# Layer one's passage between turns: a projection added sooner, key values ahead of query columns, the shift and more maxima ahead of the scores

## The chip, the cores and the metric

The kernel runs on one core of one Trainium2 chip. A core has five engines that run their own instruction streams: TensorE (PE, matmuls and transposes), VectorE (DVE), ScalarE (ACT), GpSimd (POOL) and SyncE (SP, which issues DMAs here). They meet at semaphores. The metric is the device time of one execution in microseconds (us). TensorE, VectorE and ScalarE share PSUM, eight banks of 128 x 512 f32 elements: TensorE writes a bank, another engine reads it and so makes it free.

## What is computed

Four layers, each a cross attention and a feed-forward part, act on `x` of 4 batches x 256 tokens x 256. Only layer one's attention is touched by the change. Cut to that:

```python
def _L1_xattn_ref(q, latent_kv, Wq, Wkv_expand, Wout):
    B, S, H, NH, L = (2, 256, 256, 16, 64)
    HD = H // NH
    qp = q @ Wq.T
    kv = latent_kv @ Wkv_expand.T
    k, v = jnp.split(kv, 2, axis=-1)
    # heads: (b, 16, 256, 16)
    scores = jnp.einsum('bhqd,bhkd->bhqk', qh, kh) * inv_sqrt_d
    scores = jnp.where(causal, scores, jnp.finfo(scores.dtype).min)
    attn = jax.nn.softmax(scores, axis=-1)
    out = jnp.einsum('bhqk,bhkd->bhqd', attn, vh)
    return out @ Wout.T

x = x + jnp.tanh(g_xattn[1]) * _L1_xattn_ref(_layernorm(x, axis=-1), ctx_512, ...)
```

## The kernel before

The stage of layer one's attention (its names end in `1`, its bank plan is `l1x`) takes the four batches in two turns, `i` = 0 and 1, of two batches, `s` = 0 and 1. In a turn:

- Queries (L1473) and key values (L1481) are made on TensorE. ScalarE, VectorE and GpSimd split them into bf16 parts: `query_parts1`, `key_parts1` on ScalarE (L2160) and VectorE (L2821 to L2873), the second batch's on GpSimd (L968, L970).
- TensorE turns the parts into columns (L1188): `qsT` and `ksT` for the first batch, four fills of eight transposes each, `cols` for the second, four fills of sixteen. ScalarE moves turned queries (L2040), VectorE turned keys of the first batch (L2835).
- 12 fills with scores for each batch, `max1(i, s, k)` (L1408 and the mask L1410), are reduced to maxima by VectorE (`maximum1`, L2882). Fills with k under 4 hold four heads (8 matmuls), the others two heads (4 matmuls).
- The shift made from the maxima (L2888, L2890) is turned by TensorE (`shift1`, L1188 with 32 rows), copied (L2896) and put by a DMA of SyncE (L812) into two more rows of the operands.
- `exp1(i, s, m)`, 8 fills for each batch (L1421, L1423), makes the scores once more, now less the shift; ScalarE takes the exponential (L2206); `values1` (L1439) multiplies it by the values. Then come tokens, turned heads (`turn_heads`) and the projection (`project`, L1464), which VectorE adds to x (`add_projected`, L2914). The projection of batch (0,1) is made in the second turn, after its first shift; that of (0,0) at the end of the first turn.

The order of the engines' work is written out by hand. `max_order1(i)` gives the order of maxima ahead of the scores, `AHEAD1` how many of the second batch's maxima are among them, and `rest_at1` after which scores the others go. `plan` assigns the fills of a group to banks in rotation: group M takes banks 6, 7, 4, 5; group A banks 4 and 5; B the pairs 0-1 and 2-3; V the pair 6-7. A fill waits until the one before it in its bank has been read. TensorE works in order, so what stands behind a waiting fill waits with it. VectorE fills spare time with pieces of another layer's work, `advance(largest, n)` (L2709, L2714, L2721).

Of the kernel before, what the change touches and what calls it, by code (L numbers as in the profile page):

```python
# [171 lines left out]
def flamingo_gated(nc, x, ctx_512, g_xattn, g_ffn, W_k0, b_k0, ln_gamma, ln_beta, gate_w, gate_b, expert_w, expert_b,  # L172
                   Wq1, Wkv1, Wout1, w_gate, w_up, w_down, Wq2, Wk2, gamma_raw, w12, w3, router_w, expert_bias,
                   sw1, sw2, sw3, W_router, W_sgate, Ws_gate_up, Ws_down, We_gate_up, We_down, consts, out):
    with ExitStack() as ctx:
# [350 lines left out]

        AHEAD1 = 6

# [6 lines left out]
        def max_order1(i):  # L535

            first = [("qsT", 0, k) for k in range(4)] + [("ksT", 0, k) for k in range(4)]
            for k in range(12):
                first += [("cols", 1, k // 3)] * (k % 3 == 0) + [("max", 0, k)]
            first += [("max", 1, 0), ("max", 1, 1), ("shT", 0)] + [("out", 1, 0)] * i  # L540
            return first + [("max", 1, k) for k in range(2, AHEAD1)]


        rest_at1 = {0: [6, 7], 1: [8, 9], 2: [10], 3: [11]}
        SHIFT1 = 5

        for i in range(TURNS):
            plan("l1x", i,
                 M=([6, 7, 4, 5], 1, [key for key in max_order1(i) if key[0] != "cols"]),
                 A=([4, 5], 1, [("max", 1, k) for m in rest_at1 for k in rest_at1[m]] + [("shT", 1)]  # L550
                    + [("tok", 0, 0), ("tok", 0, 1)]
                    + ([("xT", 0), ("xT", 1), ("oT", 0), ("tok", 1, 0), ("tok", 1, 1), ("out", 0), ("oT", 1)] if i == 0
                       else [("oT", 0), ("out", 0), ("AT", 0), ("AT", 1),
                             ("tok", 1, 0), ("tok", 1, 1), ("oT", 1), ("out", 1)])),
                 B=([0, 2], 2, [("q", 0), ("kv", 0), ("q", 1), ("kv", 1)] + [("cols", 1, k) for k in range(4)]
                    + [("sc", s, k) for s in range(2) for k in range(NH1 // 2)]),
                 V=([6], 2, streams([("pv",)])))
        def fills1(name, s, k=0):

            ahead = s == 0 or name == "max" and k < AHEAD1  # L560
            return pl["l1x"]["M" if ahead else "A"]

# [185 lines left out]
        def _(sp):  # L748
# [58 lines left out]
            for i in range(TURNS):  # L807
                for s in range(2):
                    f = fills1("shT", s)
                    sp.wait_ge(f.drained(i, ("shT", s)), f.read(i, ("shT", s)))  # L810
                    for r in range(2):
                        sp.dma_start(qT1[s][K1 + r:K1 + r + 1, :], shT1[s][r * NH1:(r + 1) * NH1, :])\  # L812
                          .then_inc(shift_in["l1x"].sem, 16)
                if i == 0:

                    sp.wait_ge(dense_added, 2 * T)
                    sp.wait_ge(back0_read, 2)
                    load(q3d(raw_sw[0], HC, D), sw1.rearrange("(o p) i -> p o i", p=P), "sw12")
                    load(q3d(raw_sw[1], HC, D), sw2.rearrange("(o p) i -> p o i", p=P), "sw12")
                    load(q3d(raw_sw[2], T, H_FFN), sw3.rearrange("(o p) i -> p o i", p=P), "sw3")  # L820
# [344 lines left out]
        def _(pe):  # L1165
# [224 lines left out]
            def shift1(i, s):  # L1390
                pe.wait_ge(shift_ready["l1x"].sem, shift_ready["l1x"].count(2 * i + s))
                turn(fills1("shT", s), i, ("shT", s), [(2 * NH1, t * P, sh1[s][:, t * 2 * NH1:(t + 1) * 2 * NH1]) for t in range(T)],
                     identb, BF16)

            def max1(i, s, k):
# [4 lines left out]
                elif s == 1 and k % 2 == 0 and k < 4:  # L1400
                    for n in (k // 2, 2 + k // 2):
                        pe.wait_ge(fb.drained(i, ("cols", 1, n)), fb.read(i, ("cols", 1, n)))
                f = fills1("max", s, k)
                pe.wait_ge(f.drained(i, ("max", s, k)), f.empty(i, ("max", s, k)))
# [21 lines left out]
            def values1(i, s, k):  # L1426

                fv = pl["l1x"]["V"]
                if k == 0:
                    pe.wait_ge(fv.drained(i, ("pv", s)), fv.empty(i, ("pv", s)))  # L1430
                    for n in range(AHEAD1 - 4, AHEAD1):
                        pe.wait_ge(fm.drained(i, ("max", 1, n)), fm.read(i, ("max", 1, n)))
# [56 lines left out]
            def scores1(i):  # L1489
# [10 lines left out]
                for g in range(NH1):  # L1500
# [4 lines left out]
                    if s == 0:  # L1505
                        for k in rest_at1.get(m, ()):
                            max1(i, 1, k)
# [30 lines left out]
            scores1(0)  # L1538
            turn_heads(0, 1)
            queries_turned1(1, range(2, 4))  # L1540
            key_values1(1, 1)
            scores1(1)
# [918 lines left out]
        def _(dve):  # L2461
# [414 lines left out]
            def maximum1(i, s, k):  # L2876
                nm = q3d(nmax1[s], T, NH1)
                dst, heads = (nm[:, 0, 4 * k:4 * k + 4], 4) if k < 4 else (nm[:, 1, 2 * k - 8:2 * k - 6], 2)
                f = fills1("max", s, k)
                dve.wait_ge(f.filled, f.full(i, ("max", s, k)))  # L2880
# [11 lines left out]
            def shift_turned1(i, s):  # L2892
                f = fills1("shT", s)
                dve.wait_ge(f.filled, f.full(i, ("shT", s)))
# [21 lines left out]
            def scores1(i):  # L2916
# [3 lines left out]
                for name, s, *k in max_order1(i):  # L2920
# [6 lines left out]
                    if (name, s, *k) == ("max", 0, 11):  # L2927
                        shift_rows1(0)
                for m in rest_at1:
                    for k in rest_at1[m]:  # L2930
                        maximum1(i, 1, k)
# [8 lines left out]
                if i == 0:  # L2940
# [3 lines left out]
                    weighted1(0, 1)  # L2944
                    key_parts1(1, 0)
                    query_parts1(1, 1)
                    advance(largest, 2)
                    add_projected(0, 0)
                else:
# [691 lines left out]
```

## Time and profile before

| | before |
|---|---|
| median of 3 runs | 767.08 us (763.0 to 767.57) |
| profiled execution, its own time | 758.5 us |
| its span, first to last instruction | 756.7 us |
| TensorE busy | 666.9 us (88%) |
| VectorE busy | 538.1 us (71%) |
| ScalarE busy | 351.2 us (46%) |
| GpSimd busy | 216.6 us (29%) |
| mean granted clock of TensorE | 0.966 |

The profiled execution is one execution, and its time is not that of the timed runs. In the rows below, a row of the timeline has the start, the duration, the engine, the line, what is written and read, and how many instructions were merged; in brackets is the engine's idle time ahead of it and what ended it. "issue" there means that no semaphore event explains it. A granted clock of 1.00 is TensorE's 2.4 GHz, 0.50 its 1.2 GHz.

### The profile page before, as it was taken

What the parts mean: (1) busy time and instruction counts of PE and PEld (TensorE: products, weight loads), DVE (VectorE), ACT (ScalarE), POOL (GpSimd) and SP (SyncE); (2) the same over time, 40 slices, a digit from 0 to 9 for tenths busy, and PEclk for the clock granted to TensorE, in tenths of its full rate; (3) what the DMA queues carried; (4) which work ended last, traced back from release to release, by engine and by line L of the source; (5) the groups of instructions that cost most, each with busy time, mean ns of one, the idle gap of its engine ahead of it and who ended that gap; (6) DMA issues with size and microseconds to landing.
All of it is one profiled execution on the core that took longest, in us unless ns stands there. A gap on an engine that the chain in (4) does not pass through costs nothing. (4 is left out here: it accounts for less than half of the span.)

```text
span 756.7 us, 13927 instructions
## 1 busy us (share of the span) xinstructions
PE 666.9 (88%) x4446; PEld 457.0 (60%) x4446; DVE 538.1 (71%) x1622; ACT 351.2 (46%) x620; POOL 216.6 (29%) x308
## 2 busy tenths in 40 slices
PE   8999978798997878789879999976788999999997
PEld 4644565775864656467767787653243327777776
DVE  5687988877987687888876563747986967425545
ACT  2673545565464756242115325335488794122220
POOL 1001596101100032211224652632343220523330
PEclk9999998998999999999999999997799999999999
DMA  6996521050000050000053160012000043133314
GB/s 183 343 255 126 167 85 55 3 169 1 3 3 1 2 168 1 1 0 1 29 177 123 58 217 22 29 37 78 2 3 2 3 153 79 71 103 108 93 56 173
DMA packets 55565, 60.23 MB, mean 80 GB/s; under 512 B 13847, under 2 KB 48808, under 8 KB 55496
## 3 DMA queue, kind: packets, MB, share of 16 engines
q1 hardware_dynamic: 50408, 46.02, 21.2%
q0 software_dynamic: 4848, 13.28, 5.0%
q8 instruction: 38, 0.62, 0.3%
q14 instruction: 31, 0.25, 0.1%
q10 hardware_dynamic: 240, 0.05, 0.0%
HBM read 34.92 MB, written 24.20 MB: 78 GB/s over the span
## 5 line engine op out<-in xcount | busy, mean ns | idle before, releaser
L2040 ACT ACTIVATE arenas<-psum 128x512 f32<-128x512 f32 (+6 forms) x89 | 63.1, 732 | 51.4 <-PE psum L1188 43.5
L3338 DVE TENSOR_REDUCE arenas<-psum 128x2 f32<-128x512 f32 x96 | 61.8, 684 | 12.1 <-PE psum L1791 10.7
L996 POOL TENSOR_SCALAR arenas<-arenas,small 128x1024 f32<-128x1024 f32 x8 | 9.0, 1122 | 150.2 <-DVE small L3029 150.2
L1013 POOL DMA_INDIRECT experts_l<-shared,small x30 | 29.7, 992 | 63.0 <-ACT shared L2348 52.7
L1188 PE MATMUL psum<-conb,shared 128*128 128x128 bf16 (+2 forms) x512 | 38.0, 230 | 9.6 <-issue 4.5
L2040 ACT ACTIVATE late<-psum 128x512 f32<-128x512 f32 (+1 forms) x51 | 25.6, 503 | 44.0 <-PE psum L1188 44.0
L1188 PE MATMUL psum<-con,early 128*128 128x128 f32 (+1 forms) x188 | 32.5, 284 | 14.5 <-ACT late L2040 5.1
L1188 PEld LDWEIGHTS psum<-conb,shared 128*128 128x128 bf16 (+2 forms) x512 | 33.5, 118 | 17.3 <-issue 14.8
L2395 ACT ACTIVATE early<-psum 128x1024 f32<-128x1024 f32 x32 | 32.0, 1031 | 17.3 <-PE psum L1808 17.1
L1675 PE MATMUL psum<-arenas,early 128*128 128x256 f32 x160 | 36.7, 383 | 0.8 <-DVE arenas L3492 0.8
L1188 PEld LDWEIGHTS psum<-con,early 128*128 128x128 f32 (+1 forms) x188 | 21.9, 145 | 25.0 <-ACT late L2040 8.1
L2206 ACT ACTIVATE late<-psum 128x768 f32<-128x768 f32 x32 | 25.4, 812 | 24.9 <-PE psum L1423 24.7
L1675 PE MATMUL psum<-early,late 128*128 128x256 f32 x128 | 32.3, 403 | 4.9 <-DVE early L3231 4.8
L1161 POOL DMA_INDIRECT experts_l<-late,shared x23 | 22.1, 962 | 48.6 <-DVE shared L3512 42.5
L2395 ACT ACTIVATE late<-psum 128x1024 f32<-128x1024 f32 x32 | 31.4, 1061 | 5.0 <-PE psum L1808 5.0
L2040 ACT ACTIVATE shared<-psum 128x256 f32<-128x256 f32 (+2 forms) x38 | 16.3, 429 | 37.2 <-PE psum L1188 31.9
L1675 PEld LDWEIGHTS psum<-arenas,early 128*128 128x128 f32 x160 | 29.8, 190 | 5.7 <-DVE arenas L3492 1.2
L1177 PE MATMUL psum<-conb 128*128 128x512 bf16 x128 | 31.6, 398 | 1.8 <-POOLq L904 1.8
L1188 PE MATMUL psum<-con,arenas 128*128 128x128 f32 x194 | 29.1, 279 | 4.5 <-DVE arenas L2501 2.6
L3303 DVE TENSOR_TENSOR shared<-shared,psum 128x128 f32<-128x128 f32 x30 | 8.6, 287 | 33.7 <-PE psum L1744 19.7
L1744 PE MATMUL psum<-late,shared 128*128 x120 | 32.0, 390 | 0.2 <-issue 0.2
L2882 DVE TENSOR_REDUCE arenas<-psum 128x2 f32<-128x512 f32 (+1 forms) x48 | 30.3, 683 | 2.4 <-PE psum L1410 2.3
(455 smaller groups left out, 1770.9 us busy)
## 6 DMA issues: line engine op xcount, KB each, us to landing
sorted_l<-late SPq DMA_DIRECT2D x3, 1920.0 KB, 16.5
early<-sorted_l SPq DMA_DIRECT2D x6, 645.0 KB, 5.8
early<-in_L_ffn_sw SPq DMA_DIRECT2D x3, 1024.0 KB, 9.1
late<-sorted_l SPq DMA_DIRECT2D x23, 129.0 KB, 2.1
sorted_l<-late SPq DMA_DIRECT2D x1, 2944.0 KB, 23.2
early<-in_L_ffn_We_gate_up SPq DMA_DIRECT2D x2, 1408.0 KB
early<-in_L_ffn_expert_w SPq DMA_DIRECT2D x2, 1024.0 KB, 6.8
early<-in_L_ffn_w SPq DMA_DIRECT2D x1, 2048.0 KB, 8.3
```

The costliest lines, as they stand in the source:

```text
L996: pool.tensor_scalar(ha[s][:, rows], ha[s][:, rows], c2[s][:, t:t + 1], ROUND, ALU.mult, ALU.add)
L1013: pool.indirect_dma_start(expert_rows2[p], bass.IndirectOffsetOnAxis(dest2[p][:, i:i + 1], 0), out_r2[k], None).then_inc(outs_sent[k], 16)
L1161: pool.indirect_dma_start(expert_rows, bass.IndirectOffsetOnAxis(dest[i], 0), out_r[i % OUTS], None).then_inc(out_sent[i % OUTS], 16)
L1177: pe.matmul(v, onesb, onesb.unsqueeze(1).broadcast_to([P, BANK // P, P]), start=True, stop=True)
L1188: last = pe.transpose(v[0:parts, at:at + k], src, idn[0:k, 0:k])
L1675: mm = pe.matmul(v[0:rows, half * S:(half + 1) * S], w[:, c * width + at:c * width + at + rows], xT[s][:, c * S:(c + 1) * S], start=(c == ...
L1744: mm = pe.matmul(fu.slot(p, ("up", i))[:, 0:2 * H_R2], xT_r2[i % 2][:, c * P:(c + 1) * P], w12T[:, bass.ds(which[i] * (2 * H_R2) + c * E * ...
L2040: act.activation(dst, view(v), ACT.Copy, scale=scale).then_inc(f.drained(i, key), 1)
L2206: act.activation(q3d(pexp1[m % 4], 2, S + P), q3d(v, 2, BANK)[:, :, 0:S + P], ACT.Exp, scale=HD1 ** -0.5).then_inc(fb.drained(i, ("sc", s, ...
L2395: act.activation(pexp3[w // 4][m % 4], f.slot(0, ("sc", w, m)), ACT.Exp, scale=HD3 ** -0.5)\
L2882: dve.tensor_reduce(dst, q3d(v, heads, BANK // heads), X, ALU.max, negate=True) .then_inc(f.drained(i, ("max", s, k)), 1)
L3338: dve.tensor_reduce(nm, q3d(f.slot(0, ("max", w, k)), 2, S), X, ALU.max, negate=True)\
```

## The change

Five edits, all in the order of work; no instruction is added or taken away.

1. In VectorE's stream the addition of projection (0,0) goes ahead of `query_parts1(1, 1)`.
2. In TensorE's stream `key_values1(1, 1)` goes ahead of the query columns 2 and 3 of the second turn.
3. In both turns the first shift is turned after one maximum of the second batch, not two.
4. In the first turn nine of the second batch's maxima go ahead of the scores, not six; the second turn keeps six.
5. Group M rotates over banks 6, 7, 5, 4.

```diff
-        AHEAD1 = 6
+        AHEAD1 = (9, 6)
...
-            first += [("max", 1, 0), ("max", 1, 1), ("shT", 0)] + [("out", 1, 0)] * i
-            return first + [("max", 1, k) for k in range(2, AHEAD1)]
+            first += [("max", 1, 0), ("shT", 0)] + [("out", 1, 0)] * i
+            return first + [("max", 1, k) for k in range(1, AHEAD1[i])]
...
-        rest_at1 = {0: [6, 7], 1: [8, 9], 2: [10], 3: [11]}
+        rest_at1 = ({1: [9], 2: [10], 3: [11]}, {0: [6, 7], 1: [8, 9], 2: [10], 3: [11]})
...
-                 M=([6, 7, 4, 5], 1, [key for key in max_order1(i) if key[0] != "cols"]),
+                 M=([6, 7, 5, 4], 1, [key for key in max_order1(i) if key[0] != "cols"]),
...
-                    for n in range(AHEAD1 - 4, AHEAD1):
+                    for n in range(AHEAD1[i] - 4, AHEAD1[i]):
                         pe.wait_ge(fm.drained(i, ("max", 1, n)), fm.read(i, ("max", 1, n)))
...
             scores1(0)
             turn_heads(0, 1)
+            key_values1(1, 1)
             queries_turned1(1, range(2, 4))
-            key_values1(1, 1)
             scores1(1)
...
                     key_parts1(1, 0)
+                    add_projected(0, 0)
                     query_parts1(1, 1)
                     advance(largest, 2)
-                    add_projected(0, 0)
```

The other lines of the diff only pass the turn's number to where `AHEAD1` and `rest_at1` are now one for each turn.

TensorE at the passage from the first turn to the second, before. L1464 is the projection (0,0), L1188 from `con` turns the heads, L1188 from `conb` turns query columns 2 and 3, L1481 makes the key values:

```order
L1464 MATMUL psum<-early,late 128x256 x3
L1188 MATMUL psum<-con,late 128x128 [waits bank5_drained]
L1188 MATMUL psum<-con,late 128x128 x3
L1188 MATMUL psum<-conb,shared 96x128 [waits l1x_qparts_ready,bank4_drained]
L1188 MATMUL psum<-conb,shared 96x128 x7
L1188 MATMUL psum<-conb,shared 96x128 [waits l1x_qparts_ready,bank5_drained]
L1188 MATMUL psum<-conb,shared 96x128 x7
L1481 MATMUL psum<-early,arenas 128x512 [waits bank2_drained]
```

The same place in the changed kernel:

```order
L1464 MATMUL psum<-early,late 128x256 x3
L1188 MATMUL psum<-con,late 128x128 [waits bank4_drained]
L1188 MATMUL psum<-con,late 128x128 x3
L1481 MATMUL psum<-early,arenas 128x512 [waits bank2_drained]
L1481 MATMUL psum<-early,arenas 128x512
L1188 MATMUL psum<-conb,shared 96x128 [waits l1x_qparts_ready,bank5_drained]
L1188 MATMUL psum<-conb,shared 96x128 x7
L1188 MATMUL psum<-conb,shared 96x128 [waits l1x_qparts_ready,bank4_drained]
```

The key values now stand ahead of the query columns, and the projection's bank, for which the first of these columns waits, is 5 instead of 4.

VectorE at the same place (L2873 ends the parts of the keys (1,0), L2855 is the rest of the queries (1,1), L2914 adds the projection):

```order
 L2873 COPY late<-psum 128x16x16 x2
+L2914 SCALAR_TENSOR_TENSOR xs<-psum,small,xs 128x512 [waits filled_l1xA]
 L2855 TENSOR_TENSOR late<-psum,shared 128x512 [waits l1x_q1_ready]
 L2717 TENSOR_SCALAR early<-early 128x512
```

The addition has moved ahead of four instructions of the queries and the other layer's work, with its wait for the projection.

TensorE in the second turn, the waits from the turned shift to the maxima behind the first scores, of before (only the rows that wait; L1464 is the projection (0,1), L1408 a maximum, L1421 the scores):

```order
L1188 MATMUL psum<-conb,arenas 32x128 [waits l1x_shift_ready,bank4_drained]
L1464 MATMUL psum<-early,late 128x256 [waits bank5_drained]
L1408 MATMUL psum<-arenas 128x128 [waits bank6_drained,bank2_drained]
L1408 MATMUL psum<-arenas 128x128 [waits bank7_drained]
L1408 MATMUL psum<-arenas 128x256 [waits bank4_drained]
L1408 MATMUL psum<-arenas 128x256 [waits bank5_drained]
L1421 MATMUL psum<-arenas 128x256 [waits bank0_drained,l1x_shift_in]
L1408 MATMUL psum<-arenas 128x256 [waits bank4_drained]
L1408 MATMUL psum<-arenas 128x256 [waits bank5_drained]
```

And in the changed kernel:

```order
L1188 MATMUL psum<-conb,arenas 32x128 [waits l1x_shift_ready,bank7_drained]
L1464 MATMUL psum<-early,late 128x256 [waits bank5_drained,bank4_drained]
L1408 MATMUL psum<-arenas 128x128 [waits bank4_drained]
L1408 MATMUL psum<-arenas 128x128 [waits bank6_drained,bank2_drained]
L1408 MATMUL psum<-arenas 128x128 [waits bank7_drained]
L1408 MATMUL psum<-arenas 128x256 [waits bank5_drained]
L1408 MATMUL psum<-arenas 128x256 [waits bank4_drained]
L1421 MATMUL psum<-arenas 128x256 [waits bank0_drained,l1x_shift_in]
L1408 MATMUL psum<-arenas 128x256 [waits bank4_drained]
L1408 MATMUL psum<-arenas 128x256 [waits bank5_drained]
```

One maximum has moved behind the projection, and the last fill ahead of the scores is in bank 4, where the first fill behind them goes as well; before it was in bank 5.

## Rows read from the trace of the kernel before

**Rows 1.** The page: span, two engines' busy time, granted clock in 40 slices.
```profile
span 756.7 us, 13927 instructions
...
PE 666.9 (88%) x4446; PEld 457.0 (60%) x4446; DVE 538.1 (71%) x1622; ACT 351.2 (46%) x620; POOL 216.6 (29%) x308
...
PEclk9999998998999999999999999997799999999999
```
**Rows 2.** Timeline of TensorE, the passage from the first turn to the second.
```profile
175.98 1.95 PE L1464 MATMUL psum<-early,late 128*128 128x256 f32 x8
177.77 0.60 PE L1188 MATMUL psum<-con,late 128*128 128x128 f32 x4
181.91 1.06 PE L1188 MATMUL psum<-conb,shared 128*96 128x128 bf16 x16 [3.54 <-issue]
182.90 3.41 PE L1481 MATMUL psum<-early,arenas 64*128 64x512 f32 x4
...
186.24 4.72 PE L1188 MATMUL psum<-conb,shared 128*98 128x128 bf16 x48
```
**Rows 3.** Timeline of VectorE over the same passage.
```profile
177.51 0.68 DVE L2855 TENSOR_TENSOR late<-psum,shared 128x512 f32<-128x512 f32 x1
...
181.06 0.75 DVE L2914 SCALAR_TENSOR_TENSOR xs<-psum,small,xs 128x512 f32<-128x512 f32 x1
...
187.37 0.69 DVE L2835 COPY arenas<-psum 98x1024 bf16<-98x1024 bf16 x1 [2.99 <-PE psum L1188]
...
192.09 7.47 DVE L2882 TENSOR_REDUCE arenas<-psum 128x4 f32<-128x512 f32 x12
```
**Rows 4.** Windows (busy us and count by engine, clock, DMA); a row of the first turn.
```profile
183.32:190.10 6.78, 6.78 (x40) 4.53 (x39) 3.23 (x9) 2.69 (x4) 0.00 (x0) 0.50 0.00 0
...
126.23 1.98 PE L1481 MATMUL psum<-early,arenas 64*128 64x512 f32 x4 [2.75 <-DVE late L2873]
```
**Rows 5.** Timeline: VectorE in the first turn, ScalarE and GpSimd in the passage.
```profile
130.24 2.49 DVE L2835 COPY arenas<-psum 98x1024 bf16<-98x1024 bf16 x4
...
134.21 7.46 DVE L2882 TENSOR_REDUCE arenas<-psum 128x4 f32<-128x512 f32 x12
...
182.56 1.93 ACT L2040 ACTIVATE arenas<-psum 96x1024 bf16<-96x1024 bf16 x2 [3.46 <-PE psum L1188]
...
179.90 1.16 POOL L970 TENSOR_TENSOR shared<-late,shared 128x512 bf16<-128x512 f32 x1
```
**Rows 6.** Timeline of the first turn around its first scores: VectorE, SyncE, TensorE.
```profile
142.12 1.28 DVE L2882 TENSOR_REDUCE arenas<-psum 128x4 f32<-128x512 f32 x2
143.32 0.27 DVE L2896 COPY arenas<-psum 32x256 bf16<-32x256 bf16 x1
...
143.62 1.23 SPq L812 DMA_DIRECT2D arenas<-arenas  x2
...
146.15 0.28 PE L1421 MATMUL psum<-arenas 98*128 98x256 bf16 x1 [1.81 <-DMA arenas<-arenas]
...
146.73 0.27 PE L1408 MATMUL psum<-arenas 96*128 96x256 bf16 x1
...
147.41 0.27 PE L1421 MATMUL psum<-arenas 98*128 98x256 bf16 x1
...
150.88 0.86 PE L1439 MATMUL psum<-late 128*32 128x256 f32 x16
```
**Rows 7.** Timeline of the second turn around its first scores: TensorE, VectorE.
```profile
200.45 1.99 PE L1464 MATMUL psum<-early,late 128*128 128x256 f32 x8
...
204.70 0.28 PE L1421 MATMUL psum<-arenas 98*128 98x256 bf16 x1 [0.64 <-DMA arenas<-arenas]
...
205.28 0.27 PE L1408 MATMUL psum<-arenas 96*128 96x256 bf16 x1
...
202.48 0.75 DVE L2914 SCALAR_TENSOR_TENSOR xs<-psum,small,xs 128x512 f32<-128x512 f32 x1 [1.00 <-PE psum L1464]
203.15 2.47 DVE L2882 TENSOR_REDUCE arenas<-psum 128x4 f32<-128x512 f32 x4
```

More of the change, by code:

```diff
@@ L548, in flamingo_gated @@
             plan("l1x", i,
-                 M=([6, 7, 4, 5], 1, [key for key in max_order1(i) if key[0] != "cols"]),
-                 A=([4, 5], 1, [("max", 1, k) for m in rest_at1 for k in rest_at1[m]] + [("shT", 1)]
+                 M=([6, 7, 5, 4], 1, [key for key in max_order1(i) if key[0] != "cols"]),
+                 A=([4, 5], 1, [("max", 1, k) for m in rest_at1[i] for k in rest_at1[i][m]] + [("shT", 1)]
                     + [("tok", 0, 0), ("tok", 0, 1)]
@@ L557, in flamingo_gated, with fills1 @@
                  V=([6], 2, streams([("pv",)])))
-        def fills1(name, s, k=0):
-            ahead = s == 0 or name == "max" and k < AHEAD1
+        def fills1(i, name, s, k=0):
+            ahead = s == 0 or name == "max" and k < AHEAD1[i]
             return pl["l1x"]["M" if ahead else "A"]
@@ L808, in _ @@
                 for s in range(2):
-                    f = fills1("shT", s)
+                    f = fills1(i, "shT", s)
                     sp.wait_ge(f.drained(i, ("shT", s)), f.read(i, ("shT", s)))
@@ L1391, in shift1 @@
                 pe.wait_ge(shift_ready["l1x"].sem, shift_ready["l1x"].count(2 * i + s))
-                turn(fills1("shT", s), i, ("shT", s), [(2 * NH1, t * P, sh1[s][:, t * 2 * NH1:(t + 1) * 2 * NH1]) for t in range(T)],
+                turn(fills1(i, "shT", s), i, ("shT", s), [(2 * NH1, t * P, sh1[s][:, t * 2 * NH1:(t + 1) * 2 * NH1]) for t in range(T)],
                      identb, BF16)
@@ L1402, in max1 @@
                         pe.wait_ge(fb.drained(i, ("cols", 1, n)), fb.read(i, ("cols", 1, n)))
-                f = fills1("max", s, k)
+                f = fills1(i, "max", s, k)
                 pe.wait_ge(f.drained(i, ("max", s, k)), f.empty(i, ("max", s, k)))
@@ L1505, in scores1 @@
                     if s == 0:
-                        for k in rest_at1.get(m, ()):
+                        for k in rest_at1[i].get(m, ()):
                             max1(i, 1, k)
@@ L2878, in maximum1 @@
                 dst, heads = (nm[:, 0, 4 * k:4 * k + 4], 4) if k < 4 else (nm[:, 1, 2 * k - 8:2 * k - 6], 2)
-                f = fills1("max", s, k)
+                f = fills1(i, "max", s, k)
                 dve.wait_ge(f.filled, f.full(i, ("max", s, k)))
@@ L2892, in shift_turned1 @@
             def shift_turned1(i, s):
-                f = fills1("shT", s)
+                f = fills1(i, "shT", s)
                 dve.wait_ge(f.filled, f.full(i, ("shT", s)))
@@ L2928, in scores1 @@
                         shift_rows1(0)
-                for m in rest_at1:
-                    for k in rest_at1[m]:
+                for m in rest_at1[i]:
+                    for k in rest_at1[i][m]:
                         maximum1(i, 1, k)
```

## The prediction

> **What bounds the kernel now.** I read the page first: TensorE is busy for 88% of a 756.7 us span and VectorE for 71% [rows 1]. Such shares average stages with different limits, and the change touches one stage only, the attention of layer one, so the waits are read there. The stage takes two turns of two batches: the first turn's maxima and scores run from about 131 to 170 us, the passage to the second turn from 170 to 192, the second turn from 192 to 232. Within a turn TensorE fills a bank with scores, VectorE reduces it to maxima, the shift row goes by DMA into the operands, and then TensorE makes the final scores while ScalarE takes their exponentials.
>
> Next, the timeline of TensorE in the passage [rows 2]. The reader should see 16 turned columns (L1188) at 181.91 after an idle time of 3.54 us, though the four matmuls ahead of it (turning the heads) start at 177.77. Its releaser is printed only as "issue"; the code and the times give it. The third query column goes to bank 4, which still holds the projection of batch 0, and VectorE adds that projection (L2914) at 181.06, ending at 181.81, 0.1 us ahead of TensorE's restart [rows 3].
>
> After the wait comes a second loss. The stretch from 183.32 to 190.10 has a granted clock of 0.50, the 1.2 GHz level, after TensorE had stood still from 178.37 to 181.91 [rows 4]. The four key-value matmuls take 3.41 us there and 1.98 in the first turn, at full clock; 48 transposes take 4.72 us where 16 take 1.06 at full clock, so about 3.1 [rows 2, 4]. VectorE sits idle 2.99 us for the first of them [rows 3]. Of this trace, this is the passage's limit: TensorE waits for VectorE's late addition, then VectorE waits for a slow TensorE.
>
> **The change, part by part.** All is set against the profiled execution, 758.5 us with a span of 756.7; the median of the timed runs is 767.08, 8.6 above it, and I carry the difference over unchanged.
>
> *The passage.* Two edits: VectorE adds projection (0,0) before the parts of queries (1,1), and TensorE makes key values (1,1) before query columns 2 and 3. No instruction is added. TensorE's projection starts at 175.98. In the second turn the same eight matmuls start at 200.45 and VectorE's addition follows at 202.48, so 2.03 later [rows 2, 7]. The moved addition hence starts at 178.01, where L2855 stood ready at 177.51 [rows 3]: VectorE waits 0.50 us that it did not wait before. Everything else on it up to the key copies is the same work. It was free at 187.37 - 2.99 = 184.38, so now at 184.88.
>
> TensorE meanwhile goes from turning the heads (to about 178.3) straight into key values (1.9), whose bank 2 is free since VectorE's copies ahead of 177.51, then two query columns (1.1) and four key columns (2.1). The last need ScalarE's moves of the query columns, at about 1 us each (1.93 for two) [rows 5]; that gives some 183.4 for the fourth. So the keys stand ready before VectorE comes at 184.9, and TensorE no longer decides. In the first turn the chain from the first key copy (130.24) to the first maximum (134.21) is 3.97 with nothing waited for but itself [rows 5]. The first maximum then starts at 184.88 + 0.1 + 3.97 = 188.95 instead of 192.09: **3.1 us gained**. GpSimd gets the second queries' rest 1.17 us later (178.01 + 0.67 against 177.51) and ends at 181.06 + 1.17 = 182.2 [rows 3, 5]; its reader, the second batch's first columns, is reached at about 183.4. That delay is hidden, with a cover of about 1 us.
>
> The two ends of this term: had the clock not fallen before, key values would have ended 3.41 - 1.98 = 1.43 us sooner and the first eight key transposes about 0.4 sooner, so the first maximum would have stood near 187.37 - 1.85 + 3.97 = 189.5, and the gain would be 0.5. The other end is the 3.1.
>
> The Trainium skill (TensorE: Matmul & The Clock Gate, "HAM oscillation") puts the penalty of throttled time at half of it. By that alone the 6.8 us cost 3.4 and the passage gives 3.4; the rows give 3.1, since VectorE becomes the limit, and the sum goes by them.
>
> *The first turn.* Three more maxima (6, 7 and 8 of the second batch) go ahead of the scores, where TensorE stood idle 1.81 us for the shift row's DMA; the shift's transpose, copy and DMA go one maximum earlier [rows 6]. The copy was at 143.32 behind two reductions (142.12, 1.28 for both); behind one it starts near 142.8, so the DMA (143.62) is issued near 143.05 and scores could start at 145.6. TensorE does not get there. Maxima rotate over four banks, so the fill of maximum 8 waits for the reduction of maximum 4: five reductions at 0.615 (2.47 for four in [rows 7]) and a copy of 0.27, with some 0.2 idle before maximum 1, give 145.7 when counted from 142.12; with its own 0.34 scores start at 146.1, as before (146.15). What is gained lies behind it: three maxima fewer between the first scores, at 0.34 each (two took from 146.73 to 147.41), and the waits for reduced banks that stood between them. From 146.15 to the first values at 150.88 is 4.73 [rows 6]; four scores at 0.58 (146.15 to 146.73) and three maxima at 0.34 are 3.35, and I add 0.15 for a wait or two on ScalarE. **1.2 us gained**, with 1.0 (the three maxima alone) and 1.4 as bounds. The order behind it, up to the passage, is as it was, and TensorE or what follows from it sets it all along.
>
> *The second turn.* It keeps six maxima ahead, but its shift too goes one maximum earlier, and the banks rotate 6, 7, 5, 4. Between the shift and the later maxima stands the projection that VectorE adds at 202.48, with 1.00 us of idle time ahead of it. One reduction that went ahead of that idle time now stands behind it: five instead of four from 203.15 on [rows 7]. And maximum 6, the first after scores, goes to bank 4. Before, that bank's last use was maximum 4, third in this row of reductions; now it is maximum 5, the fifth. Its reduction starts at 203.15 + 4 x 0.615 = 205.61 and takes 0.69, so TensorE's maximum 6 starts near 206.37 instead of 205.28 [rows 7]. The earlier DMA lets the scores start perhaps 0.35 before 204.70, which buys nothing: TensorE then stands at maximum 6 for 1.3 us, with all later scores queued behind. From there reductions, banks and scores follow as before. **1.1 us lost**, between 0 (if the addition frees VectorE sooner than the rows say) and 1.3.
>
> Sum: 3.1 + 1.2 - 1.1 = 3.2 us. The profile goes to 755.3 and the median to 763.9. After 232 us nothing is changed, and its first work hangs on TensorE's projection at the stage's end, so I let the gain carry to the end in full.
>
> **The rivals.**
> - *The clock was not at fault in the ordinary run.* The low stretch need not lie over the key values each time; then the passage gives 0.5, the sum is 0.6, and the time 766.5. For it: the three timed runs spread over 4.6 us. Against it: the idle time of 3.54 us is in the code's order, so some low stretch should follow it in every run.
> - *The second turn's wait is not there*, since the two bank orders come out alike: 3.1 + 1.2 = 4.3, time 762.8. The order with its waits speaks against it.
> - *Slower: the low clock moves to the maxima.* In the changed kernel TensorE waits at 183.5 to 189.1 in pieces for key copies and the reduced banks. If the clock falls there and stays low as long as before (6.8 us), some 5.3 of them lie behind 189.1. From there TensorE has nine fills at 0.34 or more and three times 16 transposes at 1.06, 6.2 us at full clock, and with half of 5.3 added it needs 8.85: the last reduction ends near 189.1 + 8.85 + 0.6 = 198.6 instead of 188.95 + 7.47 = 196.4, so 2.2 later. On top of the rival with 0.5 for the passage this is 767.08 - 0.6 + 2.2 = 768.7. It decides once the new low stretch costs more than 0.6 in a run where the old one cost nothing; against the profiled execution it would have to cost more than 3.2. Against it: the first turn has much the same pieces between its key copies and its maxima, and the slice from 132 to 151 us shows 9 tenths or more [rows 1]. The same page of the Trainium skill, under "A second HAM failure mode", speaks for it: short idle times between bank-cycled bursts make the clock swing. No stretch of the maxima in this trace agrees with it.
> - *Something later takes it back*: a low stretch of the clock in a later stage, which the page shows near 0.7 in two slices [rows 1], can come or go with the phase. It costs at most half its length, about 3.4 for one like that above.
>
> **How the numbers follow.** Likeliest (0.60): 763.9. No clock gain 0.12, no second wait 0.10, slower 0.10, later stages 0.08. Range 760.5 to 768.5: the likeliest less or plus a later low stretch of 3.4, and up to the price of the first and third rivals. Faster or slower by over 1% is 7.7 us, about what a measurement of this kernel tells from no change; no case reaches it alone, only with the spread of runs: faster 0.05, same 0.91, slower 0.04.
>
> **What would show it.** In the new profile: no idle time over 1 us between turning the heads and the first key column, key values at 1.9 to 2.0 us and a clock of 1.00 over them; first maximum of the second turn 3 us sooner relative to the passage's projection; 1.2 us less from the first turn's first scores to its first values; an idle time of about 1.3 us on TensorE after the second turn's first scores. Wrong would be a clock of 0.50 over the second turn's maxima, a wait of ScalarE or a DMA in the scores' place, or a gain in the stage that the end of the span does not show.

## The result, and the profile after

In its first comparison the changed kernel took 758.65 us (median of 20 runs, 752.71 to 763.92) and the kernel before, now also with 20 runs, 763.87 us (759.31 to 767.57); the first three of these 20 are the three of the forecast's baseline. The ratio is 0.9929, with a 95% interval from 0.9907 to 0.9952: 5.4 us faster, between 3.7 and 7.1. Forecast were 3.2 us and 763.9. The sign was right, the time lies 1.85 us below the range, and the 3.2 us that were summed lie just under the interval of this comparison. Two more comparisons of the same two kernels gave 0.9979 (0.9957 to 1.0002) and 0.9949 (0.9920 to 0.9978). The mean of the three is 0.9952, or 3.7 us. One run of those reported below, of the kernel with busy matmuls, took 1638.78 us at a granted clock of 1.00 and is left out of its ratio; what held it up no trace shows.

The page of the changed kernel (span, busy time, granted clock in 40 slices), to be read beside [rows 1]:

```profile
span 750.9 us, 13927 instructions
...
PE 663.0 (88%) x4446; PEld 454.3 (61%) x4446; DVE 536.9 (72%) x1622; ACT 350.6 (47%) x620; POOL 216.2 (29%) x308
...
PEclk9999999999999999999999999997799999999999
```

The span is 5.8 us shorter, and the two slices with an 8 in the clock's row are gone. The 5.8 us come in three pieces. The first maximum of the first turn starts at 132.31 instead of 134.21 [rows 5]: 1.90 us, and all of it stands before anything that the change moves, so no effect of the change. It is the clock's: in the kernel before TensorE was at half clock from 111.6 to 118.5, over the first queries and key values of the turn, which the change leaves as they are, and in the changed kernel's trace it was not. The first two lines are of before, the last of after (TensorE's timeline, and a window with its clock):

```profile
113.47 3.75 PE L1473 MATMUL psum<-early,arenas 128*128 128x256 f32 x8 [0.89 <-ACT arenas L2040]
113.00:117.20 4.20, 3.73 (x9) 2.55 (x9) 3.61 (x14) 0.22 (x1) 3.05 (x7) 0.50 0.00 0
...
113.02 1.97 PE L1473 MATMUL psum<-early,arenas 128*128 128x256 f32 x8 [0.94 <-ACT arenas L2040]
```

One of the two slices with an 8 is this stretch, the other is the passage. From the first maximum to the projection at the second turn's end (L1464, 221.11 us after, 226.61 before) it is 88.80 instead of 92.40: 3.60 us. From that projection to the end it is 529.8 instead of 530.1. So the stage bears on the forecast, and these 3.60 us are its gain in this pair of traces.

TensorE in the passage, in the timeline of the changed kernel, beside [rows 2]:

```profile
172.89 1.95 PE L1464 MATMUL psum<-early,late 128*128 128x256 f32 x8
174.67 0.60 PE L1188 MATMUL psum<-con,late 128*128 128x128 f32 x4
175.20 1.98 PE L1481 MATMUL psum<-early,arenas 64*128 64x512 f32 x4
177.11 2.43 PE L1188 MATMUL psum<-conb,shared 128*96 128x128 bf16 x40
179.82 1.51 PE L1188 MATMUL psum<-conb,shared 128*98 128x128 bf16 x24 [0.28 <-issue]
```

The key values follow the turned heads at once and take 1.98 us instead of 3.41; the 64 transposes of the passage are over at 181.3, 8.4 us after the projection's start, where before the last of the same 64 ended at 190.96, 15.0 us after it. The longest idle time left stands within the maxima, ahead of the second columns:

```profile
185.96 1.06 PE L1188 MATMUL psum<-conb,shared 128*96 128x128 bf16 x16 [1.48 <-issue]
```

VectorE over the same passage, beside [rows 3], and the window with its clock (the last columns are clock, DMA share and GB/s):

```profile
174.87 0.75 DVE L2914 SCALAR_TENSOR_TENSOR xs<-psum,small,xs 128x512 f32<-128x512 f32 x1 [0.37 <-PE psum L1464]
175.54 0.68 DVE L2855 TENSOR_TENSOR late<-psum,shared 128x512 f32<-128x512 f32 x1
...
181.82 2.48 DVE L2835 COPY arenas<-psum 98x1024 bf16<-98x1024 bf16 x4
...
185.77 7.46 DVE L2882 TENSOR_REDUCE arenas<-psum 128x4 f32<-128x512 f32 x12
...
174.00:185.70 11.70, 8.88 (x100) 6.67 (x98) 10.54 (x26) 7.22 (x8) 3.09 (x4) 1.00 0.00 1
```

VectorE waits 0.37 us for the projection and no longer for the keys: its key copies run in one row. (The addition now stands ahead of six instructions, not four: L2855, L2717, two of L2721, two of L2709.) From the projection's start to the first maximum it is 12.88 us instead of 16.11.

The first turn, VectorE and TensorE, beside [rows 6]:

```profile
140.84 0.27 DVE L2896 COPY arenas<-psum 32x256 bf16<-32x256 bf16 x1
141.34 5.47 DVE L2882 TENSOR_REDUCE arenas<-psum 128x4 f32<-128x512 f32 x9 [0.24 <-PE psum L1410]
...
144.23 0.27 PE L1421 MATMUL psum<-arenas 98*128 98x256 bf16 x1
...
147.80 0.86 PE L1439 MATMUL psum<-late 128*32 128x256 f32 x16
```

The scores start 11.92 us after the first maximum (11.94 before), no longer behind a DMA; from scores to values it is 3.57 us instead of 4.73.

The second turn, TensorE and then VectorE, beside [rows 7]:

```profile
194.12 1.99 PE L1464 MATMUL psum<-early,late 128*128 128x256 f32 x8
198.11 0.28 PE L1421 MATMUL psum<-arenas 98*128 98x256 bf16 x1
199.95 0.28 PE L1408 MATMUL psum<-arenas 96*128 96x256 bf16 x1 [1.10 <-DVE arenas L2882]
...
196.16 0.75 DVE L2914 SCALAR_TENSOR_TENSOR xs<-psum,small,xs 128x512 f32<-128x512 f32 x1 [1.59 <-PE psum L1464]
196.82 3.07 DVE L2882 TENSOR_REDUCE arenas<-psum 128x4 f32<-128x512 f32 x5
```

Five reductions stand behind the addition, and maximum 6 waits 1.10 us for the last of them. From first maximum to first values the second turn takes 18.34 us instead of 17.34.

### The profile page after: what moved, and what is told of

Its sections match the earlier page's. It is cut to its first block and busy times, and to the rows that moved or that the text cites. A ratio compares the mean times of both kernels' runs of the same rounds, so it can differ in the third digit from the quotient of the medians.

```text
span 750.9 us, 13927 instructions
## 1 busy us (share of the span) xinstructions
PE 663.0 (88%) x4446; PEld 454.3 (61%) x4446; DVE 536.9 (72%) x1622; ACT 350.6 (47%) x620; POOL 216.2 (29%) x308
## 5 line engine op out<-in xcount | busy, mean ns | idle before, releaser
L1188 PE MATMUL psum<-con,early 128*128 128x128 f32 (+1 forms) x188 | 32.3, 282 | 12.9 <-ACT late L2040 5.1
L1188 PE MATMUL psum<-conb,shared 128*128 128x128 bf16 (+2 forms) x512 | 37.5, 228 | 5.9 <-issue 1.8
L1188 PEld LDWEIGHTS psum<-conb,shared 128*128 128x128 bf16 (+2 forms) x512 | 33.0, 117 | 13.2 <-issue 10.7
L1188 PEld LDWEIGHTS psum<-con,early 128*128 128x128 f32 (+1 forms) x188 | 21.5, 143 | 23.5 <-ACT late L2040 8.2
L1188 PE MATMUL psum<-con,arenas 128*128 128x128 f32 x194 | 29.2, 279 | 4.5 <-DVE arenas L2501 2.6
L1317 PE MATMUL psum<-early,arenas 128*128 128x512 f32 x64 | 31.9, 621 | 0.0
```

What stands on the lines that cost most here:

```text
L1188: last = pe.transpose(v[0:parts, at:at + k], src, idn[0:k, 0:k])
L1317: pe.matmul(v, xT0[r // T][:, c * S + r % T * P:c * S + (r % T + 1) * P], ex_w[:, c * E * D + 2 * q * D:c * E * D + 2 * (q + 1) * D], star ...
```

## The experiments

The questions: are the three terms caused by what the prediction names, and is there a gain outside them? Each timed kernel of the experiments has 8 to 12 runs beside 25 to 33 of the kernel before on its chip; each has one trace. This table has, for each trace, the four stretches that the terms rest on, as differences of starts in the timelines (us): from the projection (0,0) to the second turn's first maximum; first turn, first maximum to first scores and scores to first values; second turn, the same.

| kernel | passage | first turn | second turn | ratio to before (95%) |
|---|---|---|---|---|
| before | 16.11 | 11.94 + 4.73 | 12.61 + 4.73 | |
| before, again | 16.26 | 11.95 + 4.73 | 12.43 + 4.73 | 0.9998 (0.9969 to 1.0026) |
| changed | 12.88 | 11.92 + 3.57 | 12.34 + 6.00 | 0.9929 (0.9907 to 0.9952) |
| changed, second time | 12.88 | 11.92 + 3.56 | 12.26 + 6.08 | 0.9979 (0.9957 to 1.0002) |
| changed, third time | 12.89 | 11.92 + 3.57 | 12.50 + 5.84 | 0.9949 (0.9920 to 0.9978) |
| passage only | 12.89 | 11.94 + 4.74 | 12.73 + 4.73 | 0.9957 (0.9927 to 0.9986) |
| busy matmuls | 13.48 | 11.95 + 4.73 | 12.34 + 4.80 | 0.9972 (0.9942 to 1.0002) |
| addition only | 12.88 | 11.95 + 4.73 | 14.50 + 4.73 | 0.9939 (0.9905 to 0.9974) |
| key values only | 12.56 | 11.95 + 4.73 | 12.66 + 4.73 | 0.9956 (0.9931 to 0.9982) |
| turns only | 17.32 | 11.92 + 3.56 | 12.51 + 5.83 | 1.0016 (0.9986 to 1.0046) |
| six ahead | 12.88 | 11.35 + 4.73 | 15.21 + 5.78 | one run, 758.54 us |
| banks of turn two | 12.88 | 11.92 + 3.56 | 15.09 + 5.48 | 0.9955 (0.9927 to 0.9984) |
| old second turn | 12.88 | 11.92 + 3.57 | 12.57 + 4.73 | 0.9933 (0.9902 to 0.9965) |
| the same with filler | 12.89 | 11.92 + 3.56 | 11.95 + 5.20 | 0.9918 (0.9887 to 0.9949) |

### The passage alone

```diff
             turn_heads(0, 1)
+            key_values1(1, 1)
             queries_turned1(1, range(2, 4))
-            key_values1(1, 1)
...
                     key_parts1(1, 0)
+                    add_projected(0, 0)
                     query_parts1(1, 1)
                     advance(largest, 2)
-                    add_projected(0, 0)
```

> Only the two edits of the passage (the projection added sooner, key values ahead of query columns) on the kernel before. My theory (the sum of the prediction): from the start of the projection (0,0) to the second turn's first maximum 12.9 us instead of 16.1, granted clock 1.00 between, the median 3.1 us lower. Rival (the whole change gained 2 us more than its three terms, and the excess is the passage's, since ordinary runs lose more there than the profiled one): the median 5 us lower, with the profile as above.

Measured: passage 12.89 us, and 764.79 against 769.22 us, ratio 0.9957 (0.9927 to 0.9986), 3.3 us. The trace gives the term as summed. The timed runs do not decide against a passage that is worth 5: their interval reaches from 1.1 to 5.6 us, and the medians are 4.4 apart.

### The wait kept, the clock kept up

```diff
             turn_heads(0, 1)
+            kept_busy(fb, 1, ("cols", 1, 0), 14)
             queries_turned1(1, range(2, 4))
```

> The kernel before with 14 matmuls of ones (results overwritten) in TensorE's idle time ahead of the third query column; the wait for the added projection stays. If the low clock behind the wait is what costs, the clock stays at 1.00 and the first maximum comes 13.5 us after the projection's start instead of 16.1, the median 2.6 us lower. If the wait itself costs and the clock little, 16 us and the median the same.

TensorE in the passage, in this kernel's timeline, and VectorE's first maximum (VectorE's lines are one higher in this kernel):

```profile
179.95 3.19 PE L1177 MATMUL psum<-conb 128*128 128x512 bf16 x14
183.61 1.06 PE L1188 MATMUL psum<-conb,shared 128*96 128x128 bf16 x16 [0.46 <-issue]
184.60 1.98 PE L1481 MATMUL psum<-early,arenas 64*128 64x512 f32 x4
186.51 2.88 PE L1188 MATMUL psum<-conb,shared 128*98 128x128 bf16 x48
...
191.16 1.28 DVE L2883 TENSOR_REDUCE arenas<-psum 128x4 f32<-128x512 f32 x2
```

The columns still start only when the addition is done, 5.9 us behind the projection's start as before, but key values take 1.98 and the 48 transposes 2.88 us, and the passage takes 13.48 us, 2.6 less, as expected. So 2.6 of the 3.2 us are the clock's and the other 0.6, by difference, the wait's. The clock's part is shown by the trace, since work, order and the start of the columns are the same and only useless matmuls were added. The timed ratio (0.9972, 2.2 us) cannot bear it out: its interval reaches 1, and without the run that was left out the medians are 0.5 us apart.

### One edit of the passage at a time

```diff
                     key_parts1(1, 0)
+                    add_projected(0, 0)
                     query_parts1(1, 1)
                     advance(largest, 2)
-                    add_projected(0, 0)
```

> Only VectorE's addition goes ahead of the queries' parts; TensorE's order stays. My theory: the wait of 3.54 us goes to about 0.5, the clock stays at 1.00, TensorE's columns and key values are done by 184 us of the old time, and VectorE (free at 184.9) decides as with both edits: 12.9 us and the median 3.1 lower. Rival (key values must go first to be done in time): 14 us or more and at most 2 lower.

```diff
             turn_heads(0, 1)
+            key_values1(1, 1)
             queries_turned1(1, range(2, 4))
-            key_values1(1, 1)
```

> Only the key values go ahead of the query columns on TensorE; the addition stays late. My theory: the idle time is split by 1.9 us of key values, what is left (about 1.7 us) is too little for the clock to fall, VectorE has no new wait of 0.5, and the first maximum comes about 12.4 us after the projection's start, 0.5 sooner than with both edits; the median 3.6 lower. Rival: the clock falls all the same, 14.5 us or more and the median at most 1.6 lower.

With the addition alone, a row of TensorE's timeline and the window of the following maxima:

```profile
176.66 1.06 PE L1188 MATMUL psum<-conb,shared 128*96 128x128 bf16 x16 [0.45 <-issue]
...
186.80:190.20 3.40, 3.31 (x29) 3.21 (x30) 2.29 (x4) 1.37 (x1) 1.71 (x3) 0.50 0.00 0
```

The wait is 0.45 us and the passage 12.88, the same as with both edits: the key values' move adds nothing once the addition is early. With the key values alone:

```profile
184.31 4.44 PE L1188 MATMUL psum<-conb,shared 128*96 128x128 bf16 x48 [1.63 <-issue]
...
185.40:188.70 3.30, 3.30 (x34) 3.30 (x33) 3.15 (x9) 2.90 (x4) 0.00 (x0) 0.50 0.00 0
```

The wait is split as expected and the passage takes 12.56 us, the least of all, where VectorE has no wait for the projection. But the clock did fall here, contrary to my expectation, for about 3.4 us; the keys were done in time for VectorE all the same. So the two edits are alternatives: each takes the whole gain, and together they take it once. The timed ratios, 0.9939 and 0.9956, cannot rank them.

The addition's trace shows something else. Its second turn takes 14.50 us from first maximum to scores instead of 12.61, with a clock of 0.50 from 186.8 to 190.2, within the maxima. That is the mechanism of the "slower" rival.

### The turns alone

```diff
             turn_heads(0, 1)
-            key_values1(1, 1)
             queries_turned1(1, range(2, 4))
+            key_values1(1, 1)
...
                     key_parts1(1, 0)
-                    add_projected(0, 0)
                     query_parts1(1, 1)
                     advance(largest, 2)
+                    add_projected(0, 0)
```

(against the changed kernel, so that only its maxima, shift and banks are left)

> The changed kernel without the two edits of the passage: nine maxima ahead in the first turn, the earlier shift and the banks 6, 7, 5, 4 stay. My theory: first turn's scores to values 3.6 us instead of 4.7, second turn 1.0 us longer, passage with the wait of 3.5 us and the low clock behind it (16 us) as before; the median within 0.5 us of before. Rival (the excess of 2 us comes from these edits): 2 us or more faster than before.

TensorE in the passage, the window of its low clock, and VectorE's first maximum:

```profile
179.37 1.91 PE L1188 MATMUL psum<-conb,shared 128*96 128x128 bf16 x16 [3.54 <-issue]
...
178.80:188.80 10.00, 9.43 (x57) 6.78 (x58) 5.16 (x15) 3.45 (x4) 0.00 (x0) 0.50 0.00 0
...
190.77 1.88 DVE L2882 TENSOR_REDUCE arenas<-psum 128x4 f32<-128x512 f32 x3
```

Ratio 1.0016 (0.9986 to 1.0046): the first turn's 1.2 us and the second turn's 1.0 us lost cancel, and the interval leaves the edits of the turns no gain of 2 us: at most 1.1. The wait of 3.54 us is back, and here the clock is low already over the two query columns (1.91 us instead of 1.06) and for 10 us in all; this passage costs 17.32 us. In the second trace of the kernel before it costs 16.26. So the low stretch came in each of the three traces that have the long wait on an idle TensorE, and what it costs, against the 13.48 us of the busy kernel, is 2.6, 2.8 and 3.8 us. Against the 12.88 of the changed kernel, the passage of these three is 3.2, 3.4 and 4.4 us longer.

### What parts the first turn's gain

```diff
-        AHEAD1 = (9, 6)
+        AHEAD1 = (6, 6)
...
-        rest_at1 = ({1: [9], 2: [10], 3: [11]}, {0: [6, 7], 1: [8, 9], 2: [10], 3: [11]})
+        rest_at1 = ({0: [6, 7], 1: [8, 9], 2: [10], 3: [11]}, {0: [6, 7], 1: [8, 9], 2: [10], 3: [11]})
```

> The changed kernel with six maxima ahead in the first turn too (its early shift and its banks stay). It parts the first turn's gain. My theory: the earlier shift alone lets the first scores start 0.5 to 0.6 us sooner (11.4 us from the first maximum instead of 11.9), since fewer fills stand ahead of them, and from scores to values it is 4.7 us again: the first turn gains 0.5, and the three further maxima are worth the other 0.7. Rival (the maxima ahead are the whole gain): 11.9 and 4.7 us.

The first turn's first scores and a window of the second turn's maxima:

```profile
144.46 0.28 PE L1421 MATMUL psum<-arenas 98*128 98x256 bf16 x1 [0.75 <-DMA arenas<-arenas]
...
186.30:193.00 6.70, 5.64 (x49) 5.42 (x50) 4.72 (x9) 1.87 (x1) 2.31 (x3) 0.50 0.00 1
```

The scores start 11.35 us after the first maximum and the values 4.73 after that, 16.08 in all, where it is 16.67 before and 15.49 in the changed kernel. So the earlier shift is worth 0.6 us by itself, and the three further maxima bring another 0.6: they take up the time that the earlier DMA saves, and give back 1.2 behind it. Each of the two is read from one trace. Here too the clock fell in the second turn's maxima, for 6.7 us, and the scores came 15.21 us after the first maximum.

### The second turn's loss

```diff
-                 M=([6, 7, 5, 4], 1, [key for key in max_order1(i) if key[0] != "cols"]),
+                 M=([[6, 7, 5, 4], [6, 7, 4, 5]][i], 1, [key for key in max_order1(i) if key[0] != "cols"]),
```

> The changed kernel with banks 6, 7, 4, 5 in the second turn alone; its shift stays early. If the bank order and the moved reduction share the second turn's loss, TensorE's maximum 6 waits for the fourth reduction instead of the fifth: from the second turn's first maximum to its first values 17.8 us (18.3 in the changed kernel, 17.3 before), the median 0.5 us below the changed kernel's. If the bank order alone makes it: 17.3 us and 1.0 below.

The first maximum behind the scores, and the window of the maxima ahead of them:

```profile
205.58 0.28 PE L1408 MATMUL psum<-arenas 96*128 96x256 bf16 x1 [0.58 <-DVE arenas L2882]
...
188.60:195.30 6.70, 5.95 (x51) 5.64 (x52) 4.41 (x8) 2.03 (x2) 2.31 (x3) 0.50 0.01 4
```

The wait at maximum 6 is 0.58 instead of 1.10 us, and scores to values 5.48 instead of 5.84 to 6.08. The stretch ahead of the scores is not comparable, since the clock fell in it, at a price of 2.7 us against the 12.3 of the changed kernel. What lies behind the low clock can be compared: from VectorE's addition of projection (0,1) (202.38 here) to the first values (209.74) it is 7.36 us. In the changed kernel it is 7.95 or 7.96 in all three traces, and 7.95 with six ahead, where the clock fell in the maxima too; in the two traces of the kernel before it is 6.95 and 6.77. So the bank order makes 0.6 us of the loss. That the reduction moved behind the projection makes the rest, 0.4 of the 1.0, is by difference; it was not restored alone. Restoring both:

```diff
-            first += [("max", 1, 0), ("shT", 0)] + [("out", 1, 0)] * i
-            return first + [("max", 1, k) for k in range(1, AHEAD1[i])]
+            first += [("max", 1, k) for k in range(1 + i)] + [("shT", 0)] + [("out", 1, 0)] * i
+            return first + [("max", 1, k) for k in range(1 + i, AHEAD1[i])]
...
-                 M=([6, 7, 5, 4], 1, [key for key in max_order1(i) if key[0] != "cols"]),
+                 M=([[6, 7, 5, 4], [6, 7, 4, 5]][i], 1, [key for key in max_order1(i) if key[0] != "cols"]),
```

> The changed kernel with the second turn's order and banks as in the kernel before (two maxima ahead of the shift, banks 6, 7, 4, 5); passage and first turn as changed. My theory: the second turn's loss is gone, 17.3 us from its first maximum to its first values, and the median is 1.0 us below the changed kernel's, the fastest so far. Rival (what the second turn waits for is not this order): 18.3 us and no difference.

```profile
198.22 0.28 PE L1421 MATMUL psum<-arenas 98*128 98x256 bf16 x1 [0.60 <-DMA arenas<-arenas]
...
202.95 0.75 PE L1439 MATMUL psum<-late 128*32 128x256 f32 x12
```

Scores again wait 0.60 us for the DMA, nothing waits behind them, and the second turn takes 17.30 us. The loss is gone by the trace: 1.0 us. Of this, 0.6 to 1.2 us are left over the whole stage: from its first maximum to the projection at the second turn's end it is 88.19 us, and 88.80, 89.34 and 88.92 in the changed kernel's three traces. The timed ratio is 0.9933 (0.9902 to 0.9965), 754.84 us where the changed kernel had 760.60 in the same comparison. Traces and timed runs agree that this version is faster; the size in the timed runs (5.8 us between the medians, 4.1 between the means) is more than the stage explains, and the intervals of the two ratios overlap.

### A filler in the maxima's idle time

Ahead of the second batch's first columns in the second turn, on that version:

```diff
                 for name, s, *k in max_order1(i):
+                    if i == 1 and (name, s, *k) == ("cols", 1, 0):
+                        kept_busy(fb, i, ("cols", 1, 0), 10)
                     if name == "max":
```

> The fastest version (the second turn in its old order) with 10 matmuls of ones, overwritten later, ahead of the second batch's first columns in the second turn, where TensorE waits for key copies. If short idle times there let the clock fall now and then, the filler takes that away: first maximum 12.9 us after the projection's start, clock 1.00 to the first scores 12.6 us later, median equal to that version's or up to 0.5 us lower. If the filler delays the fills, the first maximum comes later than 13.2 us and the median is higher.

```profile
180.93 2.32 PE L1177 MATMUL psum<-conb 128*128 128x512 bf16 x10
...
173.50:186.40 12.90, 11.76 (x118) 8.64 (x115) 11.67 (x28) 8.36 (x10) 3.13 (x4) 1.00 0.01 2
186.50:198.30 11.80, 10.70 (x138) 9.76 (x138) 10.61 (x21) 5.63 (x3) 1.72 (x3) 1.00 0.01 3
```

The filler delays nothing (12.89 us to the first maximum) and the clock stays at 1.00. The ratio is 0.9918 (0.9887 to 0.9949), the lowest of all measured: 755.97 against 763.55 us. But a single trace at full clock does not show that the filler keeps it there, and the two ratios, with and without it, cannot be told apart. That it helps stays open.

### The same kernels once more

> The changed kernel once more, timed beside kernels of its parts on one chip. If its gain is the sum of the three terms as its trace shows them (3.2 in the passage, 1.2 in the first turn, 1.0 lost in the second, 3.4 to 3.6 together), the ratio is near 0.9955. If there is a further gain outside the terms, it stays near 0.993, about 5 us.

> The kernel before against itself: the comparison's own spread, and a second trace of the passage. If the clock's phase makes the difference between two measured ratios of one and the same change (0.9929 and 0.9979), this ratio too may lie some tenths of a per cent from 1, and the passage shows its low stretch again, but at another place behind the idle time of 3.5 us, so between 15 and 17.5 us from projection to first maximum instead of 16.1.

> The changed kernel a third time, beside the kernel before against itself. Sum of the terms: ratio 0.9955, so 3.4 us. If there is a gain outside the terms: 0.993. In the trace the terms stay at 12.9 (projection to first maximum), 3.6 (first turn, scores to values) and 18.3 (second turn, first maximum to values) unless the clock falls within the second turn's maxima, which adds about 2 us there.

The changed kernel's stretches repeat within 0.25 us each, so the terms are firm for the executions that were traced. Its ratios do not repeat as well: 0.9979 and 0.9949, after 0.9929. The kernel before against itself gave 0.9998 with an interval of 0.3% on each side. Its median in the four comparisons was 763.87, 769.22, 761.38 and 763.55 us; the second and third are of 32 and 33 runs on one chip, 7.8 us apart, at mean clocks of 0.955 and 0.961. The window behind the wait, in the second trace of the kernel before:

```profile
184.70:191.40 6.70, 6.70 (x33) 4.16 (x34) 2.94 (x9) 3.02 (x4) 0.00 (x0) 0.50 0.00 0
```

## Why the prediction was right or wrong

**What bounds the passage: right.** Filling the wait with useless matmuls gives back 2.6 of 3.2 us, so it is mostly the low clock behind the wait, as the windows had it, and less the wait. The two parts follow the working: VectorE waits for the projection (0.37 us against 0.50 forecast), and then it decides.

**The passage's term: right,** 3.23 against 3.1. The lower end of 0.5, a low stretch that stays away in ordinary runs, did not occur in any of the three traces with the wait. One thing was not seen: either edit alone brings it all. And one trace was taken for the usual case: the other two traces with the wait give 3.4 and 4.4 on the same measure.

**The first turn: right,** 1.16 + 0.02 against 1.2, with scores at the same place and the gain behind them, as forecast. The prediction booked it all on the three further maxima; the trace with six ahead has 0.6 us of it from the earlier shift alone.

**The second turn: right in place and mechanism,** 1.10 us of wait at maximum 6 where 1.3 were forecast, 1.00 lost in the stretch against 1.1. The bank order is 0.6 of it.

**The sum against its own time: right.** 3.23 + 1.18 - 1.00 = 3.4, with 0.2 in the smaller waits behind it 3.6; forecast 3.2. Its ratio, 1 - 3.2/764 = 0.9958, is near the mean of the three measured (0.9952).

**The step that failed** is the one at the head of the change's part: "the median of the timed runs is 767.08, 8.6 above it, and I carry the difference over unchanged". That median was of three runs, and two of the three are the slowest of the 20. With 20 runs it is 763.87, 5.4 above the profiled execution and not 8.6, so 3.2 of the 5.3 us by which 763.9 missed are the baseline's. The range had 3.4 us for the clock's luck in later stages, but counted from a center that was itself a draw; set around 763.87 - 3.2 = 760.7, its lower end is 757.3 and the measured 758.65 lies inside, by 1.4. (Its upper end, 768.5, is 0.2 below the 768.7 at which the third rival was priced, and which it was said to hold.) The runs show how large such a draw is: among the changed kernel's first 20 runs, one at a mean clock of 0.973 took 752.71 us and one at 0.952 took 763.37. At half clock for 2 x (1 - 0.973) x 750.9 = 41 us and 73 us of their spans, they differ by 33 us of low clock and 10.7 us of time, about a third of a us for each. The clock is not all of it: two of the 20, both at 0.961, took 758.62 and 763.92. Where the draw falls, the traces show: the stretch from the projection at the second turn's end to the end of the span, which no edit touches, took from 529.8 to 543.2 us in the fourteen traces, and 530.1 in the profiled execution that the forecast was set against.

**The remaining 2.0 us** (763.87 - 3.2 = 760.7 against 758.65) are not settled. The edits of the passage alone gave 3.3 us (1.1 to 5.6), those of the turns alone nothing. The second and third comparison gave 1.6 and 3.9 us instead of 5.4. The three traces with the wait put the passage at 3.7 us on average, where 3.1 were summed: that would be 0.6 of the 2.0. And the profiled pair had 1.90 us of difference from a low stretch of the clock ahead of everything changed, so the clock's luck can make such a size; that it did so in the medians of 20 runs is not shown.

**The rivals.** "The clock was not at fault" fell. "The second turn's wait is not there" fell. "The low clock moves to the maxima" did occur: of eight traces in which the early addition ends the passage's wait, and without filler, three (addition only, six ahead, banks of turn two) have it, at 1.9 to 2.9 us, where I had 2.2 for a chance of 0.10. It did not decide the sign, since the passage gains 3.2 to 4.4 each time, but it takes most of the gain: from the stage's first maximum to the projection at its end these three took 91.08, 92.23 and 91.10 us, against 92.40 before and 88.80 to 89.34 in the changed kernel's three traces, none of which has it. How often it comes in the timed runs no trace shows. The rule named beside it in the Trainium skill (TensorE: Matmul & The Clock Gate, "A second HAM failure mode"), that short idle times between bank-cycled bursts make the clock swing, agrees with the three windows at 0.50 above; the other five traces kept 1.00. "Something later takes it back" did not occur in the profiled pair (529.8 against 530.1 us behind the stage); in the changed kernel's second and third trace the same stretch took 534.3 and 533.3 us, 3 to 4 more, and in the second trace of the kernel before 530.9.

## What to carry to other kernels

Price an idle time of TensorE by what runs behind it at half clock, and test it by filling it with useless matmuls: that parts the wait from the clock in one run. When a bank rotation or the work ahead of a fixed addition is shifted by one, look up which fill was the last in the bank that the next stage's first fill takes; the bank step was worth 0.6 us here, and with one reduction more behind the addition 1.0. And an absolute time of a kernel with many low-clock stretches is a weak thing to forecast: three runs were 3.2 us off the median of 20, and medians of over 30 runs on one chip were 7.8 us apart. Forecast the difference, and take for its size more than one trace of the kernel before.

## What was not expected of the hardware

The clock fell after a wait of only 1.63 us (key values alone: 0.50 from 185.4 to 188.7, with TensorE busy all through that stretch), and in the kernels with the addition early it fell in the second turn's maxima in three traces of eight, behind idle times of at most 1.5 us at a time (at 186.8, 186.1 and 188.5, each within the 1.5 us ahead of the second columns; the same idle time stands in the five others). After the wait of 3.54 us the low stretch was 6.8, 6.8 and over 10 us long in three traces, and began before or after TensorE's restart: the same order of work met the clock at different places.
